# Silu of z by ScalarE's own table, more C products on VectorE and one small product on GpSimd, in a fused Mamba and RWKV layer

## The reference

```
h  = layernorm(x)
xh, z = split(h @ W_in);  B, C, dt = parts of xh @ W_x
delta = softplus(dt @ W_dt + b_dt)
for each of 16 state columns n:  s_n[t] = exp(delta * A_n) * s_n[t-1] + (delta * xh) * B_n[t]
y   = sum over n of C_n[t] * s_n[t]  +  D * xh
res = (y * silu(z)) @ W_out + h;   x2 = x + layernorm(res) * ln_g + ln_b
h2  = layernorm(x2);  xr, xk = mixes of h2 with the token before it
out = x2 + sigmoid(xr @ W_r.T) * ((relu(xk @ W_k.T) ** 2) @ W_v.T)
```

## Time and profile before

| | us |
|---|---|
| three runs | 942.05, 943.9, 944.43; median 943.9 |
| the profiled execution | 944.42, with a span of 942.6 |
| VectorE busy | 900.9 |
| GpSimd busy | 889.1 |
| TensorE busy | 864.2 |
| ScalarE busy | 847.9 |
| steps, gate product to gate product | from 52.0 to 57.5 |

### The profile page before, as it was taken

How to read it: one execution, slowest core, us unless ns; L and a number is a source line. 1 busy time by engine, 2 the same in 40 slices (tenths; PEclk the granted TensorE clock), 3 DMA queues, 4 the chain that set the end, 5 groups by cost and what they waited for, 6 DMA issues and landing times.

```text
span 942.6 us, 15838 instructions
## 1 busy us (share of the span) xinstructions
PE 864.2 (92%) x5024; PEld 688.7 (73%) x5024; DVE 900.9 (96%) x985; ACT 847.9 (90%) x2064; POOL 889.1 (94%) x399
## 2 busy tenths in 40 slices
PE   8757679999999899989999899998999999999998
PEld 5545567877878587787868678786778768778876
DVE  4899989999999999999999999999999999999896
ACT  5886988989999999998999999999999999978875
POOL 4999999999999999999999989999999999999970
PEclk9987898999999999999999999999999999999999
DMA  7445435462534644455463644446354354446231
GB/s 222 156 177 204 175 138 204 179 235 104 210 157 161 239 164 172 183 178 166 174 248 147 224 148 160 179 179 248 125 210 179 143 198 179 157 160 223 91 101 45
DMA packets 49938, 163.60 MB, mean 174 GB/s; under 512 B 5248, under 2 KB 33152, under 8 KB 33600
## 3 DMA queue, kind: packets, MB, share of 16 engines
q1 hardware_dynamic: 48528, 161.27, 46.2%
q0 software_dynamic: 512, 1.31, 0.5%
q10 hardware_dynamic: 816, 0.02, 0.1%
HBM read 153.15 MB, written 9.44 MB: 172 GB/s over the span
## 4 chain that ended last, share of the span: by engine, by line
PE 46%; ACT 28%; DVE 15%; issue 9%; DMA 1%; POOL 0%; POOLq 0%; DVEq 0%; SPq 0%; ACTq 0%
PE w_ps L1326 10%; ACT da_ps L654 10%; PE y_ps L1317 9%; PE w_ps L1350 6%; DVE da_ps L1033 5%; PE w_ps L1359 4%; PE w_ps L1362 4%; DVE hg L1049 3%; DVE hg L1033 3%; PE w_ps L1465 3%; DVE hg L1040 2%; PE w_ps L1368 2%; ACT xn_tok L591 2%; ACT h_tok L591 2%; ACT zs L715 2%
## 5 line engine op out<-in xcount | busy, mean ns | idle before, releaser
L542 POOL TENSOR_TENSOR dbx<-u,b_ring 128x1024 f32<-128x1024 f32 x255 | 599.4, 2380 | 4.7 <-DVE hg L1033 4.6
L654 ACT ACTIVATE da_ps<-delta,a_neg 128x512 f32<-128x512 f32 x512 | 340.0, 684 | 23.9 <-DVE hg L1040 7.3
L555 POOL TENSOR_TENSOR hg<-hg,c_ring 128x1024 f32<-128x1024 f32 x122 | 290.4, 2381 | 8.5 <-ACT carry L660 6.7
L1317 PE MATMUL y_ps<-ident,hg 128*128 128x128 f32 x2048 | 264.3, 279 | 9.2 <-POOL hg L555 9.0
L1317 PEld LDWEIGHTS y_ps<-ident,hg 128*128 128x128 f32 x2048 | 241.7, 145 | 35.9 <-issue 17.8
L1033 DVE TENSOR_TENSOR_SCAN da_ps<-da_ps,carry,dbx 128x512 f32<-128x512 f32 x203 | 249.8, 1271 | 4.3 <-ACT da_ps L654 4.1
L1033 DVE TENSOR_TENSOR_SCAN hg<-da_ps,carry,dbx 128x512 f32<-128x512 f32 x181 | 220.3, 1263 | 1.4 <-ACT carry L660 1.2
L1040 DVE TENSOR_TENSOR hg<-da_ps,c_ring 128x1024 f32<-128x1024 f32 x68 | 82.3, 1210 | 0.2
L1049 DVE TENSOR_TENSOR hg<-da_ps,c_ring 128x512 f32<-128x512 f32 x130 | 82.3, 673 | 0.0
L1033 DVE TENSOR_TENSOR_SCAN da_ps<-da_ps,dbx 128x512 f32<-128x512 f32 x64 | 75.8, 1213 | 3.3 <-ACT da_ps L654 2.8
L1326 PE MATMUL w_ps<-xnT_ring,w_in 128*128 128x512 f32 x120 | 61.4, 636 | 16.0 <-ACT xT L696 14.1
(11 more groups left out here) (212 smaller groups left out, 1333.0 us busy)
## 6 DMA issues: line engine op xcount, KB each, us to landing
c_ring<-bc_rows_dram SPq DMA_DIRECT2D x64, 1024.0 KB, 4.7
b_ring<-bc_rows_dram SPq DMA_DIRECT2D x63, 1024.0 KB, 6.7
xres<-in_L_attn_x_in_dram SPq DMA_DIRECT2D x16, 512.0 KB, 4.8
x_tok<-in_L_attn_x_in_dram SPq DMA_DIRECT2D x15, 512.0 KB, 5.9
out_dram<-r_out SPq DMA_DIRECT2D x14, 512.0 KB, 3.2
bc_rows_dram<-bc_rows SPq DMA_DIRECT2D x64, 16.0 KB, 5.4
w_in<-in_L_attn_W_in_dram SPq DMA_DIRECT2D x2, 256.0 KB, 4.3
x_tok<-in_L_attn_x_in_dram SPq DMA_DIRECT2D x2, 256.0 KB, 4.6
```

The lines of the kernel that those rows point to most:

```text
L542: pool.tensor_tensor(dbx[:, n % X_RING, :, :], u[:, ip, :, :], b.to_broadcast([P, KH, LC]), ALU.mult).then_inc(s["dbx_done"], 1)
L555: pool.tensor_tensor(part, part, c_of(n).to_broadcast([P, KH, LC]), ALU.mult).then_inc(s["g_pool"], 1)
L654: act.activation(da_of(n, h), delta[:, ip, h, :], ACT.Exp, scale=a_neg[:, h, n:n + 1]).then_inc(s["da_ready"], 1)
L1317: last = pe.matmul(y_tok[:, b, h * P:(h + 1) * P], hg[:, n % H_RING, h, b * P:(b + 1) * P], ident[:, :], is_transpose=True, start=n == 0 a ...
```

## The change

It has four parts. **Silu**: ScalarE takes silu(z) from its own table straight out of the bank, so VectorE's two products and the halving of the weights go. The set with silu is loaded, both parts are made and the set with exp and ln is loaded, all at place 21; the set with exp and tanh is loaded as before after softplus, so a step has four loads. **C products**: column 9 is split in even steps, and column 9 takes the place of column 3 in odd ones, so both kinds have the same nine split columns. **First norm**: the four products of mean and rs become one of 128 x 4 on GpSimd at column 12. **Order**: most places, TensorE's columns and the banks are given anew; the gate moves from place 8 to 10, and z0 and z1 on TensorE from columns 2 and 3 to column 6.

The diff, cut to its core (left out: names of semaphores, the split of tanh_r's loop into its caller, which keeps the order):

```diff
...
 HEAD_COLS = 2
-SPLITS = [[0, 2, 5, 6, 8, 11, 12, 14], [0, 2, 3, 5, 6, 8, 11, 12, 14]]
+SPLITS = [[0, 2, 5, 6, 8, 9, 11, 12, 14], [0, 2, 5, 6, 8, 9, 11, 12, 14]]
 LAST_SPLIT = [5, 6, 8, 9, 11, 12]
...
 LN_EXP = "natural_log_exp_and_others"
+SILU = "silu_and_others"
 SOFTPLUS = "softplus"
 EXP_TANH = "exp_and_others"
...
-ACT_TURN = dict(prev=0, norm1=3, hT1=3, xnT1=4, xnT0=4, hT0=5, bc=6, k0=9, sp=10, z0=11, z1=11, gT0=11, gT1=12,
-                sum1=15, sq1=16, x0=18, tanh=19, ln_exp=20, rs1=22, x1=22, sq20=22, sq21=23, rs2=23, k1=24, square=24,
-                sum30=25, sum31=27, sum3_set=28, sq3=28, rs3=29, ev0=31, ev1=31, norm3=31)
-VEC_TURN = dict(mix1=5, mix0=6, gate=8, z0=12, z1=16, u0=17, u1=22, x20=24, x21=25, v0=31, v1=31)
-PE_TURN = dict(hT1=0, xnT1=1, xnT0=1, hT0=2, dt0=2, bc=2, dt1=2, k0=2, z0=2, z1=3, gT0=3, gT1=4, r0=5, x0=5, r1=6,
-               x1=6, wo1=7, wo0=7, k1=7, xa1=9, xa0=9, xD=10, v0=12, v1=12, xo0=13, xo1=13)
-BANK = dict(x0=0, r1=2, r0=1, hT0=1, bc=2, dt1=0, k0=1, gT1=0, x1=0, gT0=0, hT1=1, v0=1, wo0=2, wo1=1, z1=2, k1=0,
-            v1=2, dt0=2, xnT0=2, xnT1=0, z0=1)
+ACT_TURN = dict(prev=0, norm1=3, hT1=3, xnT1=4, xnT0=4, hT0=5, bc=8, k0=9, sp=10, gT0=12, gT1=12, sum1=15, sq1=16,
+                x0=17, tanh=18, silu=21, rs1=23, x1=21, sq20=22, sq21=23, rs2=23, k1=24, square=24, sum30=27,
+                sum31=27, sum3_set=27, sq3=28, rs3=29, ev0=31, ev1=31, norm3=31)
+VEC_TURN = dict(mix1=5, mix0=7, gate=10, u0=16, u1=21, x20=25, x21=25, v0=30, v1=31)
+PE_TURN = dict(hT1=1, xnT1=1, xnT0=1, hT0=2, dt0=2, bc=2, dt1=2, k0=2, z0=6, z1=6, gT0=3, gT1=4, r0=2, x0=4, r1=5,
+               x1=6, wo1=7, wo0=7, k1=7, xa1=9, xa0=9, xD=13, v0=11, v1=11, xo0=13, xo1=13)
+POOL_TURN = dict(nr1=12)
+BANK = dict(hT0=1, v1=2, r1=2, hT1=1, v0=1, bc=2, gT0=2, wo0=2, x1=0, dt1=0, z0=1, gT1=2, xnT0=2, xnT1=0, k0=1, wo1=1,
+            x0=0, dt0=2, r0=1, z1=2, k1=0)
...
+            def scale_mean(count):
+                need(pool, ln_rs[1], count)
+                pool.tensor_tensor(nr[1][:, :], nm[1][:, :], rs[1][:, :], ALU.mult).then_inc(ln_nr[1], 1)
             def step(t, par, pre=False, scan=False, mid=False, end=False, late=False, more=False):
                 nxt = 1 - par
                 for n in range(NS):
+                    if more and t >= 0 and n == POOL_TURN["nr1"]:
+                        scale_mean(t + 3)
...
                 act.activation(rs[ln][:, :], lv[ln][:, :], ACT.Exp, scale=-0.5).then_inc(ln_rs[ln], 1)
-                if ln in nr:
+                if ln == 3:
                     need(act, ln_rs[ln], count)
...
-                def tanh_z(v, m, to):
+                def silu_z(v, m, to):
                     need_ready(act, v, f"z{m}")
-                    act.activation(zs[:, to, 2 * m:2 * m + 2, :], by_block(bank(v, f"z{m}")), ACT.Tanh).then_inc(s[f"tanh{m}_done"], 1)
-                def tanh_r(mark, c):
+                    act.activation(zs[:, to, 2 * m:2 * m + 2, :], by_block(bank(v, f"z{m}")), ACT.Silu).then_inc(read_sem(v, f"z{m}"), 1)
...
                     if t == 0 and place == 0:
-                        act.preload_act_table_set(EXP_TANH)
+                        act.preload_act_table_set(SILU)
                         for m in range(2):
-                            tanh_z(-1, m, par)
+                            silu_z(-1, m, par)
+                        act.preload_act_table_set(LN_EXP)
...
                         if at(mark + "tanh"):
                             if late:
                                 act.preload_act_table_set(EXP_TANH)
-                            tanh_r(mark, c)
+                            for v in range(2):
+                                tanh_r(mark, c, v)
                             if late:
                                 act.preload_act_table_set(LN_EXP)
+                    if pre and not start and at("silu"):
+                        act.preload_act_table_set(SILU)
+                        need(act, s["gated_done"], t)
+                        for m in range(2):
+                            silu_z(t, m, nxt)
+                        act.preload_act_table_set(LN_EXP)
...
                             scale_x(m)
-                    for m in range(2):
-                        if pre and not start and at(f"z{m}"):
-                            need(act, s["gated_done"], t)
-                            tanh_z(t, m, nxt)
-                    if pre and not start and at("ln_exp"):
-                        act.preload_act_table_set(LN_EXP)
...
-            def halve_w_z():
-                dve.wait_ge(s["w_z_loaded"], 16)
-                dve.tensor_scalar(w_in[:, :, D:], w_in[:, :, D:], 0.5, None, ALU.mult).then_inc(s["w_z_halved"], 1)
...
-                def silu(v, m, to):
-                    need_ready(dve, v, f"z{m}")
-                    need(dve, s[f"tanh{m}_done"], v + 2)
-                    part = zs[:, to, 2 * m:2 * m + 2, :]
-                    dve.scalar_tensor_tensor(part, part, 1.0, by_block(bank(v, f"z{m}")), ALU.add,
-                                             ALU.mult).then_inc(read_sem(v, f"z{m}"), 1)
...
-                    if t == 0 and place == 1:
-                        for m in range(2):
-                            silu(-1, m, par)
-                    for m in range(2):
-                        if pre and not start and at(f"z{m}"):
-                            silu(t, m, nxt)
...
                         if start:
-                            pe.wait_ge(s["w_z_halved"], 1)
+                            pe.wait_ge(s["w_z_loaded"], 16)
...
```

More of the change, by code:

```diff
@@ L197, in mamba_rwkv_layer @@
                        + [da_ps[:, m, :] for m in range(DA_BANKS)])
-        names = """w_in_loaded w_x_loaded w_dt_loaded w_bc_loaded w_z_loaded w_z_halved a_loaded w_loaded mu_loaded w_r_in w_kv_in ffn_turned ffn_set ident0 ident_done flags_done
+        names = """w_in_loaded w_x_loaded w_dt_loaded w_bc_loaded w_z_loaded a_loaded w_loaded mu_loaded w_r_in w_kv_in ffn_turned ffn_set ident0 ident_done flags_done
             a_exped a_set omu_set setup_pe setup_ev
@@ L202, in mamba_rwkv_layer @@
             xn_done bc_rows_done
-            u0_done u1_done tanh0_done tanh1_done
+            u0_done u1_done
             scan_done carry_saved carry_split da_ready dbx_done g_pool g_vec y_added
@@ L710, in hT_in, with tanh_r @@
                     act.activation(h_of[:, m, 1:LC + 1], b[:, :], ACT.Copy).then_inc(mixed_prev[m], 1)
-                def tanh_z(v, m, to):
+                def silu_z(v, m, to):
                     need_ready(act, v, f"z{m}")
-                    act.activation(zs[:, to, 2 * m:2 * m + 2, :], by_block(bank(v, f"z{m}")), ACT.Tanh).then_inc(s[f"tanh{m}_done"], 1)
-                def tanh_r(mark, c):
+                    act.activation(zs[:, to, 2 * m:2 * m + 2, :], by_block(bank(v, f"z{m}")), ACT.Silu).then_inc(read_sem(v, f"z{m}"), 1)
+                def tanh_r(mark, c, v):
                     to = x_tok if mark else r_out
@@ L720, in tanh_r @@
                         need(act, s["out_stored"], 16 * c)
-                    for v in range(2):
-                        need_ready(act, t, f"{mark}r{v}")
-                        act.activation(to[:, 2 * v:2 * v + 2, :], by_block(bank(t, f"{mark}r{v}")), ACT.Tanh,
-                                       scale=0.5).then_inc(read_sem(t, f"{mark}r{v}"), 1)
+                    need_ready(act, t, f"{mark}r{v}")
+                    act.activation(to[:, 2 * v:2 * v + 2, :], by_block(bank(t, f"{mark}r{v}")), ACT.Tanh,
+                                   scale=0.5).then_inc(read_sem(t, f"{mark}r{v}"), 1)
                 def at(stage):
@@ L1111, in step @@
                         first_norm(0)
-                        halve_w_z()
                     if start and at("second"):
```

## The result

The change made the kernel slower: 960.15 us, median of 4 runs (959.56 to 961.78), against 943.31 (942.05 to 944.43). The ratio is 1.0185, with an interval from 1.017 to 1.020. The forecast was 949 with a range from 938 to 960. The sign and the named wait came out; the size did not: 16.8 us more than the kernel before, where 5 were forecast. The profiled execution took 959.56 us with a span of 957.8, which is 15.2 more than the span before.

The account below looks back on a forecast made before the run. VectorE was taken to set the pace, busy 220.1 of 222.0 us in four stretches. +6.0 us over eleven stretches, -0.5 in the first three steps and -0.5 to the last chunk made +5.0 on 944.4: 949 us, range 938 to 960.

Parts of the forecast that it names:

- The decisive step: Load, silu, silu, load at place 21 after split column 9 make VectorE wait at column 12; 1.6 us an ordinary stretch.
- Rival 1: At exp (12,0) VectorE's work covers the batch, so stalls go and the kernel is faster: 934 to 938 us; chance 0.27.
- rival 2: Half of the walked stalls appear, a stretch costs 55.5 us as before, no change: 942 to 946 us; chance 0.20.
- The steady sum: Four stretches take 224.2 against 222.0 us: +0.55 a stretch, +6.0 over the eleven from chunk 3 to chunk 14.
- The start: First three steps: less VectorE and GpSimd work against silu stalls and one load more, -0.5 us, between -4 and +3.
- a load more stands ahead of the first carry: In the first three steps, one more ScalarE table load before the first carry, inside their -0.5 us.
- I cost this at nothing: TensorE's z0 and z1 moved to column 6: ready 2 and 0.3 us before their silu, so no cost.
- The last stretch: The stretch to the last chunk was put at -0.5 us.
- rival 4: Silu on ScalarE dearer than tanh: +0.2 us a step, 952 us; chance 0.47 together with the walked stalls.
- Rival 5: A table switch holds ScalarE as long again as its 1.28 us row: 20 us, or 969; chance 0.06 with rival 3.
- The mean product: First norm's product of four numbers on GpSimd: 0.15 us, its wait costing nothing; ScalarE saves 0.76 us a step.
- rival 3: TensorE late with z1, wo0 or wo1: 1 us a step gives +15, or 964 us; chance 0.06 with Rival 5.

Follow-up runs that it names:

- experiment 11: Changed kernel with tanh in place of the first chunk's silu of z, so no load back to exp and ln in the start: 958.46 us, ratio 1.0172.
- experiment 6: Changed kernel, all four loads kept, with half of z's matmuls left out from step 0 on: 966.83 us, ratio 1.0236.
- experiment 5: Changed kernel without the silu set's load at place 21, tanh in silu's place, and half of z's matmuls left out from step 0 on: 938.92 us, ratio 0.995.
- experiment 4: Kernel before with one more table load, the silu set loaded at place 20 ahead of exp and ln and never used: 959.32 us, ratio 1.0181.
- 1: Changed kernel with the silu set's load taken out at place 21 and tanh in silu's place: 954.85 us, ratio 1.0135.
- 3: Changed kernel with the first norm's four mean products back on ScalarE at place 23: 967.8 us, ratio 1.0272.
- 9: Changed kernel with chunk 1's copy of x and its square one place later, behind column 12's exponentials: 960.01 us, ratio 1.0187.
- 10: Changed kernel with the third norm's mean product also on GpSimd instead of ScalarE: 958.92 us, ratio 1.0177.
- experiment 12: Kernel before with the first and third norm's mean products on GpSimd instead of ScalarE: 952.15 us, ratio 1.0101.

## Why the prediction was right or wrong

**The decisive step held.** From the end of C9 the walk had exp (12,0) done after 7.2 us and VectorE ready after 6.5. The trace has the carry at 567.63 and the scan at 574.86, 0.76 idle for a walked 0.7. The later waits were walked as 0.45, 0.2 and 0.1 to 0.2, and are 0.25, 0.25 and 0.15. Over four stretches the walk gives 6.2 us of stalls, and VectorE was idle 6.2. That the sums are equal is partly luck: in the batch entry's first stretch it idled 2.5 where 2.1 were walked, in the next two 1.45 where 1.6 were. Rival 1 (the cover suffices) and rival 2 (half of the stalls) fell to these rows.

**The steady sum was still 2.9 short** (+8.9 for +6.0). Two terms did it. VectorE's work fell by 1.1 in four stretches and not by 1.8. Part of that is how an idle engine counts: two scans in a row take a slot of 1.18 us each, but one with a wait behind it takes its full length (574.86 and 1.29 and 0.25 make 576.40), 0.1 more for each of three or four waits a stretch. That is worked out from the rows and has no run of its own. And I took 0.3 off four stretches for rounding, which the trace does not give back. Both together are 1.0 in four stretches, 2.7 over eleven.

**The start was the largest miss**: -0.5 forecast with bounds of -4 and +3, +3.9 measured, outside the bounds. Two steps of the prediction failed there. The first is "a load more stands ahead of the first carry", which I named and did not walk: that load is on the path in full (experiment 11: 1.4 us less of wait at the first exponential). The second is TensorE, "I cost this at nothing": in the first two batches z is late, and as the prediction says of that case, the lateness stands ahead of exp (12,0). ScalarE waits 1.13 us for z1 in the first and 0.67 and 1.07 for both parts in the second, and VectorE 2.26 us (at 69.9) and 2.61 (at 123.7) behind them. With half of z's matmuls (experiment 6) these waits of VectorE are 1.29 and 0.76, with the load in place. TensorE's granted clock is 0.81 on average from 36 to 98 us and 0.86 from there to the second gate, against 1.00 in the steady stretches; the kernel before has 0.82 and 0.85 there, so it is not the clock that changed; what changed is that the exponentials now stand behind z.

**The last stretch** was put at -0.5 and is +2.3. I had counted the work that falls and none of the stalls, though the step has the batch like every other: its waits of 0.76, 0.24 and 0.25 are 1.25 of the 2.3, and experiment 5, where the batch runs through, takes 1.37 off the stretch. The waits behind them look larger, 1.34 for a carry and 0.53 and 0.31 for hT copies, but the kernel before has 1.22 and 0.32 of them in its own last stretch, so they add only 0.6. VectorE's busy time makes up the rest: 48.31 instead of 50.25, which with the 2.4 us of scans that now lie ahead of gate 14 is +0.5 and not less.

**The price of silu** held: two take 1.08 us with a slot of 1.10, and two tanh in the same place 1.06 with a slot of 1.07 (experiment 5); rival 4 is out. **The load** also: 1.30 from its start to the next instruction, at both loads of the batch. Rival 5, the longer switch, is out; the section What ACT_TABLE_LOAD costs of the Trainium skill's page ScalarE: Activation LUTs agrees with the trace on the load (1283 ns) and not on the drain, since experiment 4's two loads in a row stand 1.29 us apart and added 1.1 us a step.

**The mean product** took 0.20 us instead of 0.15 and waited for nothing. Its worth was underestimated: I counted it into ScalarE's balance only; it is 7.6 us in the changed kernel.

**TensorE** was costed at nothing with a cover of 0.3 us for z1. In the steady steps the cover is 0.5 and it held; in the first two batches it did not, so rival 3 came in there and nowhere else. What I had not seen of the steady steps is the reverse: it is the next bound, 0.44 us behind the load, so that the load's own share of the loss could not be had by taking it out. The work of the load is 15 x 1.28 = 19 us; without it the kernel gains 5.3.

Settled by runs: the wait at column 12 comes from the batch and has two feeders of nearly equal length (1, 5, 6); ScalarE's order after it has no slack to hide work moved later (3, 9) and little to gain from work taken out (10); the start's load (11), z in the first two batches (6), and that the last stretch pays for its batch (5). Open: the 0.9 us of the wait at 49.3 us, why the carry of the last stretch is late in both kernels, and whether another order of TensorE alone would help.

## What to carry to other kernels

Moving work off the busiest engine pays only if what is put in its place is not on the path that feeds it: 0.3 us a step came off VectorE (0.45 were forecast), and 1.3 us a step of table load went in front of the exponential that it reads next. Count a just-in-time producer by its gapless run: once ScalarE has no gap between two hand-overs, moving one of its instructions within the run changes nothing, adding one costs most of its length, and taking one away gives only the distance to the next chain. Walk the first and last steps as carefully as the steady one; here they held 6 of 15 us. And before a wait is put down to a change, look for it in the kernel before.

## What I had not expected of the hardware

With less work TensorE ran slower. With half of z's matmuls gone and the load in place, TensorE idled 1.76 and then 1.98 us within 8 us, busy 5.62 of them, and its granted clock fell from 1.00 to 0.72 in the 6 us that followed; eight matmuls took 3.13 instead of 1.89 us. Without the load the same half left the matmuls at their speed and the kernel at 938.92 us.

A 128 x 4 product of two tensors takes 0.20 us on GpSimd (up to 0.29 in experiment 12), against 2.37 for 128 x 1024.
